# An attention stage on one Trainium2 core: PE waits once for two banks of raw scores instead of once for each

## The reference, cut to what matters

```python
x = x + 0.5 * _L0_ffn_ref(_layernorm(x), ...)          # 8 experts, top 2
x = x + _L0_attn_ref(_layernorm(x), q_w, k_w, v_w, o_w)
x = x + 0.5 * _L0_ffn_ref(_layernorm(x), ...)
x = x + 0.5 * _L1_ffn_ref(_layernorm(x), ...)
x = x + _L1_attn_ref(_layernorm(x), ...)               # linear, no scores
x = x + 0.5 * _L1_ffn_ref(_layernorm(x), ...)

def _L0_attn_ref(x, q_w, k_w, v_w, o_w):               # x: 2 x 2048 x 512
    q = (x @ q_w.T).reshape(b, s, 16, 32).transpose(0, 2, 1, 3)
    k = x @ k_w.T                                      # one key and value head
    v = x @ v_w.T
    scores = jnp.einsum('bhqd,bkd->bhqk', q, k) * 32 ** -0.5
    attn = jax.nn.softmax(scores, axis=-1)
    out = jnp.einsum('bhqk,bkd->bhqd', attn, v)
    return out.transpose(0, 2, 1, 3).reshape(b, s, 512) @ o_w.T
```

## Time and profile before

| | |
|---|---|
| median of 3 runs | 4774.67 us (4774.04 to 4779.06) |
| the profiled execution, device time | 4780.76 us |
| its span, first to last instruction | 4779.2 us, mean granted TensorE clock 0.974 |
| busy: PE, PEld | 4579.4 us (96%), 3492.0 us (73%) |
| busy: DVE, ACT, POOL | 2885.2 us (60%), 2108.4 us (44%), 2255.8 us (47%) |
| the attention stage | its first `maxi` starts at 936.0 us, its last at 2485.3 us |

### The profile page before, as it was taken

The page is one execution under the profiler, slowest core; times in us unless marked ns, Lnnn a source line. Parts: engine busy times, 40 slices in busy tenths (PEclk is TensorE's granted clock), DMA queues, the critical chain, the costliest instruction groups (busy, mean ns, idle before and its releaser), DMA issues. The chain is left out here.

```text
span 4779.2 us, 82403 instructions
## 1 busy us (share of the span) xinstructions
PE 4579.4 (96%) x27966; PEld 3492.0 (73%) x27967; DVE 2885.2 (60%) x5285; ACT 2108.4 (44%) x4111; POOL 2255.8 (47%) x1724
## 2 busy tenths in 40 slices
PE   6999996999999999999999699999899999999999
PEld 4888885666666666666667488888788877778888
DVE  6222225789999999999974733322455548754444
ACT  4222224467666676766762422222322235533222
POOL 0545434178888888888881054543111007500000
PEclk8999998899999999999999799999899999999999
DMA  7232326657777777777765734433522112250110
GB/s 220 87 104 93 104 78 235 238 111 147 146 147 146 146 146 146 146 149 150 148 135 154 223 108 136 130 124 108 177 67 71 58 49 82 71 198 27 36 36 27
DMA packets 246003, 585.98 MB, mean 123 GB/s; under 512 B 30816, under 2 KB 85088, under 8 KB 221152
## 3 DMA queue, kind: packets, MB, share of 16 engines
q0 software_dynamic: 62064, 317.23, 29.5%
q1 hardware_dynamic: 183536, 263.86, 16.7%
HBM read 263.27 MB, written 121.63 MB: 81 GB/s over the span
## 5 line engine op out<-in xcount | busy, mean ns | idle before, releaser
L1401 POOL TENSOR_TENSOR attend_pairs<-attend_pt 128x1024 f32<-128x1024 f32 x512 | 1257.5, 2471 | 200.4 <-ACT attend_pt L1366 199.7
L1414 DVE TENSOR_REDUCE attend_mx<-attend_am_ps 128x1 f32<-128x512 f32 x2048 | 1252.0, 679 | 125.0 <-PE attend_am_ps L1274 121.8
L1366 ACT ACTIVATE attend_pt<-attend_sc_ps 128x512 f32<-128x512 f32 x2048 | 1040.3, 617 | 286.0 <-PE attend_sc_ps L1262 285.9
L1274 PE MATMUL attend_am_ps<-attention_kst,attend_qst 96*128 96x512 f32 x2048 | 859.4, 425 | 10.2 <-DMA attend_qst<-q_parts 10.1
L1262 PE MATMUL attend_sc_ps<-attend_qst,attention_kst 98*128 98x512 f32 x2048 | 816.6, 400 | 1.5 <-ACT attend_pt L1366 1.3
L1665 PE MATMUL ffn_gu_ps<-ffn_y_hi,ffn_w 128*128 128x512 f32 (+1 forms) x1584 | 566.6, 367 | 3.1 <-DVE ffn_y_lo L1795 3.0
L1274 PEld LDWEIGHTS attend_am_ps<-attention_kst,attend_qst 96*128 96x128 f32 x2048 | 393.2, 192 | 241.1 <-DVE attend_mx L1414 123.5
L1665 PE MATMUL ffn_gu_ps<-ffn_y_lo,ffn_w 128*128 128x512 f32 (+1 forms) x1584 | 566.0, 366 | 0.0
L759 DVE TENSOR_TENSOR expert_ac<-expert_gu_ps,expert_gl 128x512 f32<-128x512 f32 x142 | 98.2, 692 | 747.6 <-ACT expert_gl L706 710.3
L1288 PE MATMUL attend_pv_ps<-attend_pt,attention_v 128*32 128x256 f32 x8192 | 495.1, 382 | 0.0
L1262 PEld LDWEIGHTS attend_sc_ps<-attend_qst,attention_kst 98*128 98x128 f32 x2048 | 389.9, 191 | 87.1 <-ACT attend_pt L1366 11.7
(11 more groups left out here) (329 smaller groups left out, 7472.8 us busy)
## 6 DMA issues: line engine op xcount, KB each, us to landing
attend_pairs<-attend_pairs POOLq DMA_DIRECT2D x189, 1024.0 KB
weights_raw<-experts_dram POOLq DMA_DIRECT2D x76, 512.0 KB
ys<-expert_ob SPq DMA_DIRECT2D x142, 256.0 KB
attend_qst<-q_parts SPq DMA_DIRECT2D x192, 128.0 KB, 4.0
yn<-route_yb SPq DMA_DIRECT2D x64, 256.0 KB
ffn_xb<-x SPq DMA_DIRECT2D x64, 256.0 KB, 2.9
keyvalue_xb<-x SPq DMA_DIRECT2D x64, 256.0 KB, 2.7
weights_lo<-experts_dram SPq DMA_DIRECT2D x24, 512.0 KB
```

Source lines behind the costliest of these rows:

```text
L1274: pe.matmul(am[:, bank, :], qst[0:KROWS, n % 2, h * HALF + hd, :], kst[0:KROWS, o:o + 4 * P], start=True, stop=True).then_inc(am_rdy, 1)
L1366: act.activation(pt[:, u % RING, g * 4 * P:(g + 1) * 4 * P], sc[:, s % SBANKS, :], ACT.Exp, scale=HD ** -0.5).then_inc(p_rdy, 1)
L1401: pool.tensor_tensor(pairs[:, slot(half, j), :], pt[:, 2 * p % RING, :], pt[:, (2 * p + 1) % RING, :], ALU.add).then_inc(pair_rdy, 1)
L1414: dve.tensor_reduce(mx[:, hh, block:block + 1], am[:, am_slot["max", a] % MBANKS, :], AX.X, ALU.max).then_inc(mx_rdy, 1)
```

## The change

`am_bank` is replaced by `am_free(k)`, which holds the wait alone. The `maxi` of an even number a now waits for the banks of both slot k and slot k + 1; the `maxi` of the odd number behind it waits for nothing. Since DVE reads the banks in order, the wait for slot k is left out wherever k - 4 and k - 3 are both maxima, and the wait for slot k + 1 alone stands. `turn` waits as before. Nothing else is moved: the matmuls and their order are the same.

```diff
-            def am_bank(use):
-
-                k = am_slot[use]
+            def am_free(k):
+
                 if k >= MBANKS:
                     kind, which = am_use[k - MBANKS]
                     pe.wait_ge(mx_rdy if kind == "max" else mT_kept, which + 1)
-                return k % MBANKS
...
-                bank = am_bank(("max", a))
+                k = am_slot["max", a]
+                if a % 2 == 0:
+                    if k + 1 - MBANKS < 0 or am_use[k + 1 - MBANKS][0] != "max" or am_use[k - MBANKS][0] != "max":
+                        am_free(k)
+                    am_free(k + 1)
```

More of the change, by code:

```diff
@@ L1271, in maxi @@
                     pe.wait_ge(q_in[n % 2][h], (n // 2) * 48 + 48)
-                bank = am_bank(("max", a))
+                k = am_slot["max", a]
[3 more added lines that the diff above has]
+                    am_free(k + 1)
                 o = (n // QT) * S + block * 4 * P
-                pe.matmul(am[:, bank, :], qst[0:KROWS, n % 2, h * HALF + hd, :], kst[0:KROWS, o:o + 4 * P],
+                pe.matmul(am[:, k % MBANKS, :], qst[0:KROWS, n % 2, h * HALF + hd, :], kst[0:KROWS, o:o + 4 * P],
                           start=True, stop=True).then_inc(am_rdy, 1)
@@ L1279, in turn @@
                 pe.wait_ge(neg_rdy, half + 1)
-                bank = am_bank(("turn", half))
-                pe.transpose(am[0:HALF, bank, 0:P], neg[:], const["ident"][:]).then_inc(mT_rdy, 1)
+                k = am_slot["turn", half]
+                am_free(k)
+                pe.transpose(am[0:HALF, k % MBANKS, 0:P], neg[:], const["ident"][:]).then_inc(mT_rdy, 1)
             def values(u):
```

## The result

| | before | changed |
|---|---|---|
| median, us | 4776.86 (4774.04 to 4779.72, 4 runs) | 4864.64 (4862.69 to 4867.43, 4 runs) |
| ratio | | 1.0183, 95% interval 1.0167 to 1.0199 |
| the profiled execution, its span | 4780.76, 4779.2 | 4864.76, 4863.1 |

The change makes the kernel slower by 88 us in the medians and by 84 between the two profiled executions. The forecast was 4854, within 4838 to 4886.

What follows compares the result with a forecast made beforehand. The prediction took PE as the bound, with DVE near. 62 transpose batches at 0.47 us and 187 others at 0.27 gave 79.6 us, which against the median 4774.7 made 4854 us, range 4838 to 4886.

Steps and rivals of the forecast that it cites:

- Ordinary batch, +0.27: Batch without transpose: load 6 waits for reduction 3, 0.38 us late less 0.12 of lead, so 0.27 us longer.
- the load's lead: A load runs ahead of its matmul, so in each batch it may be 0.12 us late and cost nothing.
- Batch with add-ups: DVE, 0.12 us late there, would come in time: +0.27 us; bound 0.12 more in 62 batches, 7 us.
- Transpose batch, +0.47: In 62 batches load 6 also waits for DVE's copy, so `values` comes at 1518.35 instead of 1517.88: +0.47 us.
- Removed waits, 0 to 13 us: Satisfied waits gone before `maxi`: taken as 0, far bound 13 us at no more than 13 ns a pair.
- the lead-in: Opening stretch with `maxi` alone, where DVE sets the pace: change there 0, still 34.3 us.
- The lead was used: Rival at `values`: the lead isn't given back after PE empties, slower still at 4884 us; chance 0.10.
- The clock stayed at 1.00: Rival: the clock falls as PE stands empty twice in transpose batches, 360 us more, 5214; chance 0.05.
- The rule of the Trainium skill: Short idle spells between groups cycling through PSUM banks make the clock swing; by it the clock rival would occur.
- Faster and unchanged: Rivals: waits themselves cost, 13 us saved, 4761, chance 0.02; nothing changes, lateness hidden or old waits kept, 4775, chance 0.02.

Runs made afterwards that it cites:

- the run with the pair at 4 alone: Changed kernel with the pair of waits only at maxima 4 and 5 of each batch, all others waiting singly: 4805.98 us, ratio 1.0054.
- The run with the late target and all its waits: Changed kernel with every odd maximum waiting for its own bank again, even ones still waiting for the next bank too: 4861.06 us, ratio 1.0172.
- halved reductions: DVE reduces only 256 of 512 scores per bank: kernel before 4751.03 us, changed kernel 4763.71; single waits in lead-in alone 4757.28, waits in twos there alone 4757.51.

## Why the prediction was right

The direction, the mechanism and, to within 11 us of the medians (4864.6 against 4854), the size held: PE gains on DVE within a batch, load 7 has 0.08 us to spare, and load 6 with load 7's target has not.

- **Ordinary batch, +0.27.** 6.07 predicted and 6.07 measured. Load 4 late by 0.13, load 6 by 0.39, 0.12 of it covered by the load's lead, `values` 0.79 behind load 7: each as written. That load 4's lateness has no effect can't be told in this kernel, where load 6 waits anyway; the run with the pair at 4 alone has it, at 0.02 us in an ordinary batch.
- **Batch with add-ups.** That DVE would no longer come late there was right: over the batches of the middle its first reduction starts 0.54 after load 0, and the price is 0.27 again.
- **Transpose batch, +0.47.** Measured 6.64 in the mean instead of 6.10, so +0.54. The mis-sized term is the end of load 6's wait: I took 0.05 from the copy's end to the load and it is 0.12, since the load carries two waits. 62 x 0.065 = 4 us, shown by leaving one of the two out. The prediction had priced the second wait at 13 ns, from the bound for a satisfied one.
- **Removed waits, 0 to 13 us.** 0 was right. The bound from the earlier trace rows was no price of the maxima's waits.
- **The range.** At its upper end the prediction adds 2 us for the batches with add-ups, after it had bounded them by 7 itself; the measured time is far from that end, so nothing hangs on it.
- **The sum.** 79.6 predicted for the batches, 84.5 measured from first to last `maxi`; 4 of the 5 are the second wait, some 0.4 the lead-in. The 3.3 us behind it, which the prediction has no term for, stand with a granted clock of 0.89 instead of 0.96 in batches whose code the change does not touch. Whether they are the change's doing stays open. The run with the late target and all its waits has 42.1 us there, as the kernel before. But all seven kernels in which load 6 waits for two banks have 42.1 to 45.4 us there, and of the six others five have 40.4 to 40.6, each in one trace. The medians differ by 88, of which the profiles leave 4 to the spread between executions. That the total came within 11 us of the forecast is thus no luck of errors that cancel: the batches give 80 and 84, and the rest is small.
- **The rivals.** The lead was used: `values` came 0.79 behind load 7 and no later. The clock stayed at 1.00 through the middle of the stage, though the loader stands idle before load 4 and load 6 of every transpose batch (0.54 and 0.39 us in the one above) and PE's own records have a gap of 0.22 us before the first of them. The rule of the Trainium skill that the prediction weighed ("TensorE: Matmul & The Clock Gate", "A second HAM failure mode: psum-queue depth-cycling") did not come true there. In the lead-in with halved reductions, 0.50 against 0.89 in two pairs of kernels, short waits for banks do go with a low clock, but it stays low and does not swing as in that section. The full kernel's lead-in is at 0.50 with either kind of wait, before and after, so it had nothing to lose there. Faster and unchanged were wrong.

## What to carry to other kernels

A wait whose target is already reached cost this PE nothing that these runs can show; what counts is how early the engine asks. Merging the waits of two buffers into one at the first of them moves the first one's target by a whole buffer, so compare the two engines' paces within the burst, not their busy shares over the stage: the fourth bank was worth 0.27 us of 5.80 in an ordinary batch and 0.54 of 6.10 in one with a transpose. Where the slower engine has an extra task, try it behind the burst and not in it; that was worth 12 us here, and the removed waits nothing.

## What the runs showed of the hardware

- A load of a stationary operand that waits late for one semaphore starts 0.05 us after the end of the DVE instruction that raises it; with two waits on it, in the transpose batches, 0.12.
- After PE has run empty, the next load of a `maxi` follows after 0.34 instead of 0.47 us, once. A load that came 0.12 us late cost 0.02 in the ordinary batches of the run with the pair at 4 alone (5.82 against 5.80).
- 744 removed waits changed the time by a factor of 1.0001 (0.9992 to 1.001), and those of the odd maxima put back changed 1633.6 us to 1633.7.
- With halved reductions and waits in twos, whose loads come in twos with gaps of 0.35 to 0.38 us between them and whose matmuls start 0.43 to 0.46 apart, the clock stayed at 1.2 GHz through the whole lead-in (26.0 us); with single waits it rose within it (20.6 us), in two kernels each. Gaps of up to 0.54 us between loads in the transpose batches of the changed kernel did not bring a clock of 2.4 GHz down.
- In the batches behind the last `maxi`, the same code took 40.4 to 40.6 us at a granted clock of 1.00, 42.1 or 42.2 at 0.96, and 45.4 at 0.89.
